# A sparse graph-attention kernel: batch order, gather columns and store placement near its end

## What is computed

```
h  = relu(layernorm(x)) @ W                       # 8192 x 128
e  = leaky_relu(h@a_src [:,None] + h@a_dst [None,:], 0.2)
e  = where(adj > 0, e, -9e15)
out = x + softmax(e, axis=1) @ h                  # a row without neighbours gets the mean of h
```

## Time and profile before

| | before |
|---|---|
| median of 3 runs, us | 804.62 |
| profiled execution, us (its span) | 803.09 (801.3) |
| busy: PE, DVE, ACT, POOL | 64%, 75%, 66%, 64% |
| DMA | 299.31 MB, mean 374 GB/s |
| last instruction on DVE before the final store starts | 793.30 us |

### The profile page before, as it was taken

The page is one execution under the profiler, slowest core; times in us unless marked ns, Lnnn a source line. Parts: engine busy times, 40 slices in busy tenths (PEclk is TensorE's granted clock), DMA queues, the critical chain, the costliest instruction groups (busy, mean ns, idle before and its releaser), DMA issues.

```text
span 801.3 us, 8973 instructions
## 1 busy us (share of the span) xinstructions
PE 516.1 (64%) x1855; PEld 233.0 (29%) x1855; DVE 602.0 (75%) x3125; ACT 527.0 (66%) x371; POOL 512.4 (64%) x522
## 2 busy tenths in 40 slices
PE   3786566677667667666657766676766666756521
PEld 3762223233222233232222222232322122222221
DVE  7957568766876768777779778777776798768984
ACT  3889667676766667676767767677666767676300
POOL 4753776665657665677667666656777656667771
PEclk9799756656765675876785676667667677676655
DMA  8999999999999999999999999999999999999410
GB/s 333 424 393 407 401 403 410 407 406 413 405 407 413 404 407 394 405 396 400 390 400 404 390 402 410 395 409 398 390 382 403 380 406 396 404 380 385 137 37 15
DMA packets 40904, 299.31 MB, mean 374 GB/s; under 512 B 11053, under 2 KB 14035, under 8 KB 24465
## 3 DMA queue, kind: packets, MB, share of 16 engines
q1 hardware_dynamic: 22976, 276.83, 85.5%
q0 software_dynamic: 15328, 17.58, 7.0%
q10 hardware_dynamic: 2544, 4.33, 1.6%
HBM read 304.31 MB, written 8.65 MB: 391 GB/s over the span
## 4 chain that ended last, share of the span: by engine, by line
DMA 70%; ACT 10%; issue 8%; DVE 8%; PE 3%; POOLq 0%; ACTq 0%; DVEq 0%
DMA adj_buf<-in_adj 69%; ACT mask_buf L467 9%; DVE x_all L821 3%; PE banks L1018 1%; DVE stats L560 1%; PE banks L1049 1%; ACT work L431 1%; PE banks L1008 1%; DMA x_all<-in_x 1%; ACT gathered L446 0%; DVE mv_all L564 0%; ACT work L441 0%; DVE newton L577 0%; DVE newton L579 0%; DVE rstd L581 0%
## 5 line engine op out<-in xcount | busy, mean ns | idle before, releaser
L467 ACT ACTIVATE mask_buf<-adj_buf,minus_half 128x2048 bf16<-128x2048 int32 x252 | 490.4, 1994 | 205.9 <-DMA adj_buf<-in_adj 205.4
L361 POOL DMA_INDIRECT gathered<-table,index x448 | 448.3, 1001 | 242.1 <-issue 145.5
L1049 PE MATMUL banks<-mask_buf,bit_ident 128*128 128x512 bf16 x1024 | 388.9, 528 | 103.5 <-ACT mask_buf L467 102.7
L1049 PEld LDWEIGHTS banks<-mask_buf,bit_ident 128*128 128x128 bf16 x1024 | 107.9, 124 | 329.2 <-ACT mask_buf L467 191.6
L821 DVE SCALAR_TENSOR_TENSOR x_all<-gathered,weight,x_all 128x128 f32<-128x128 f32 x512 | 157.7, 348 | 7.2
L636 DVE MAX8 words<-banks 128x8 f32<-128x512 f32 x64 | 44.7, 699 | 122.6 <-PE banks L1049 122.6
L1047 PE MATMUL banks<-key_rows,ones_b 3*128 3x512 bf16 x64 | 32.3, 504 | 124.0 <-ACT mask_buf L467 123.5
L1090 PE MATMUL banks<-x_all,one_hot 128*128 128x128 f32 x128 | 42.5, 433 | 17.5 <-DVE x_all L821 17.4
L1047 PEld LDWEIGHTS banks<-key_rows,ones_b 3*128 3x128 bf16 x64 | 6.1, 95 | 145.7 <-ACT mask_buf L467 144.2
L640 DVE MAX8 words<-rest 128x8 f32<-128x512 f32 x64 | 44.5, 695 | 2.2
L638 DVE MATCH_REPLACE8 rest<-words,banks 128x512 f32<-128x512 f32 x64 | 43.6, 681 | 0.0
(11 more groups left out here) (162 smaller groups left out, 536.1 us busy)
## 6 DMA issues: line engine op xcount, KB each, us to landing
adj_buf<-in_adj SPq DMA_DIRECT2D x128, 2048.0 KB, 18.7
gathered<-table,index POOLq DMA_INDIRECT x448, 6.4
table<-gathered ACTq DMA_DIRECT2D x4, 1040.0 KB, 14.7
x_all<-in_x SPq DMA_DIRECT2D x3, 1024.0 KB, 11.0
out<-x_all SPq DMA_DIRECT2D x2, 1280.0 KB, 23.2
x_all<-in_x SPq DMA_DIRECT2D x2, 512.0 KB, 5.3
out<-x_all SPq DMA_DIRECT2D x1, 1024.0 KB, 26.3
w_gathered<-table,w_index POOLq DMA_INDIRECT x24, 5.8
```

The costliest lines, as they stand in the source:

```text
L361: nc.gpsimd.indirect_dma_start(g_cols[buf][:, k, :], None, table, bass.IndirectOffsetOnAxis(index[:, buf, k:k + 1], 0), bounds_check=N, oo ...
L467: nc.scalar.activation(mask_buf[:, u], adj_buf[:, u], ACT.Sign, bias=minus_half[:]).then_inc(mask_ready, 1)
L1049: ins = mm(bank, bit_ident[:, h * PART_BITS + c], mask_buf[:, u, c * BIT_COLS:(c + 1) * BIT_COLS], start=False, stop=(h == PARTS - 1 and c ...
```

## The change

`BY_TILE` takes in batch 29. From batch 28 on (`CATCH_UP`) DVE sums batch i-2 and no longer i-3: batch 28 holds two sums, 25 and 26, and batch 31 none. The logits of batches 26 to 29 stand alone behind `make_records` of the batch after; ACT's softmax of batch i-2 stands behind unit 4 (in batch 28 behind unit 3). The last pair of units is loaded as one unit and two halves, each half masked and packed by itself. SP's stores wait for the last half. In batch 31 each tile has six gather columns and none is shared; neighbours from the seventh on make the node wide. After the loop, logits and placing stand between the steps of sums. Groups end with batches 10, 21 and 31 (before 9, 19, 31), and the first two groups' wide gathers are issued in threes over three batches. `wide_logits` waits for the sums first; `wide_sum` divides at its end and not at its start.

```diff
...
+CATCH_UP = 28
+WIDE_PARTS = ((0, 3), (3, 6), (6, 9))
+GROUP_ENDS = (10, 21, 31)
...
+BY_TILE = (29, 30, 31)
...
+        w_acc = [work[:, 1, 0, :], work[:, 1, 1, :]]
...
+            def load_part(i, u, lo, hi, loaded):
+                row = rows_of(adj, i * BATCH + u // PARTS, 1)[:, 0, :]
+                at = u % PARTS * PART
+                sp.dma_start(adj_buf[:, u, lo:hi], row[:, at + lo:at + hi]).then_inc(loaded, 16)
...
+                for u in range(0, UNITS - 2 if i == LAST else UNITS, 2):
...
+            sp.wait_ge(mask_ready, LAST * UNITS - 1)
+            load_part(LAST, UNITS - 2, 0, PART, adj_loaded[UNITS // 2 - 1])
+            sp.wait_ge(mask_ready, LAST * UNITS)
+            for h in range(2):
+                load_part(LAST, UNITS - 1, h * PART // 2, (h + 1) * PART // 2, end_loaded[h])
+            sp.wait_ge(end_loaded[1], 16)
...
-                    gather(buf, OWN, SLOTS, end_gathers_done[0])
...
-                    if i == GROUP_ENDS[g] + 3:
-                        wide_gather(g)
-            wide_gather(GROUPS - 1)
+                    for part, (lo, hi) in enumerate(WIDE_PARTS):
+                        if i == GROUP_ENDS[g] + 2 + part:
+                            wide_gather(g, lo, hi)
+            wide_gather(GROUPS - 1, 0, MORE + 1)
...
+            def mask_last():
+
+                act.wait_ge(part_packed, LAST * UNITS)
+                for h, signal in enumerate((end_masked, mask_ready)):
+                    act.wait_ge(end_loaded[h], 16)
+                    half = slice(h * PART // 2, (h + 1) * PART // 2)
+                    nc.scalar.activation(mask_buf[:, UNITS - 1, half], adj_buf[:, UNITS - 1, half], ACT.Sign,
+                                         bias=minus_half[:]).then_inc(signal, 1)
...
-                    mask(i, u)
-                    if u == 3 and i >= SUM_LAG:
+                    if i == LAST and u == UNITS - 1:
+                        mask_last()
+                    else:
+                        mask(i, u)
+                    if u == 3 and SUM_LAG <= i <= CATCH_UP:
                         softmax(i - SUM_LAG)
+                    if u == (3 if i == CATCH_UP else 4) and i >= CATCH_UP:
+                        softmax(i - 2)
                     for g in range(GROUPS - 1):
                         if u == 5 and i == GROUP_ENDS[g] + 7:
                             wide_softmax(g)
-                    if u == 6 and i == LAST:
-                        softmax(LAST - 2)
...
+                if i == LAST:
+                    ours, shared = (slice(0, OWN), slice(OWN, SLOTS)) if lo == 0 else (slice(SHARED, SLOTS), slice(0, SHARED))
+                    v.memset(valid[:, par, lo, shared], 0.0)
+                    done.add(v.tensor_scalar(valid[:, par, lo, ours], top[:, lo, 0:OWN], float(MEAN_KEY), None, ALU.is_ge))
+                    settled()
+                    next(beside, None)
+                    v.scalar_tensor_tensor(own, top[:, B, 0:OWN], -float(MEAN_KEY), skip[:, B, 0:OWN],
+                                           ALU.add, ALU.add).then_inc(index_ready, 1)
...
+                    v.tensor_copy(ninth[:], top[:, :, OWN])
+                    v.tensor_copy(rec[:, ring, :, 0:MORE], top[:, :, OWN:OWN + MORE])
+                    v.tensor_scalar(unfit[:, 4], top[:, :, OWN + MORE], float(EXP_BIAS), None, ALU.is_ge)
...
+            def later(rounds, steps):
+
+                for _ in range(rounds):
+                    yield
+                yield from steps
...
-                for k in range(SLOTS):
+                first = SHARED if i == LAST and lo else 0
+                for k in range(first, first + (OWN if i == LAST else SLOTS)):
...
-                dve.wait_ge(w_gathers, 16 * (MORE + 1) * (g + 1))
-                settled()
-                done.add(v.tensor_scalar(w_tmp[:, 0], w_gathered[:, :, D_COL], w_rec[:, REC_S:REC_S + 1], None, ALU.add))
-                settled()
-                done.add(v.scalar_tensor_tensor(w_tmp[:, 1], w_tmp[:, 0], ALPHA, w_tmp[:, 0], ALU.mult, ALU.max))
-                settled()
-                done.add(v.tensor_tensor(w_tmp[:, 0], w_tmp[:, 1], w_valid[:], ALU.mult))
-                settled()
-                done.add(v.tensor_scalar(w_tmp[:, 1], w_valid[:], 1.0, MASKED, ALU.subtract, ALU.mult))
-                settled()
-                done.add(v.tensor_tensor(w_score[:, 0:MORE], w_tmp[:, 0], w_tmp[:, 1], ALU.add))
-                settled()
 
                 dve.wait_ge(sums_closed, g + 1)
                 sums = banks[:, sums_banks[g], 0:SUMS]
                 done.add(v.tensor_copy(w_score[:, MORE:MORE + 1], sums[:, F:F + 1]))
+                dve.wait_ge(w_gathers, 16 * MORE * (g + 1))
+                settled()
+                done.add(v.tensor_scalar(w_tmp[:, 0], w_gathered[:, :, D_COL], w_rec[:, REC_S:REC_S + 1], None, ALU.add))
+                settled()
+                done.add(v.scalar_tensor_tensor(w_tmp[:, 1], w_tmp[:, 0], ALPHA, w_tmp[:, 0], ALU.mult, ALU.max))
+                settled()
+                done.add(v.tensor_tensor(w_score[:, 0:MORE], w_tmp[:, 1], w_masked[:], ALU.add))
                 settled()
                 v.tensor_reduce(w_m[:, 0:1], w_score[:], AX.X, ALU.max, negate=True).then_inc(w_logits, 1)
 
+                dve.wait_ge(w_x_gathered, 16 * (g + 1))
...
+                v.tensor_scalar(w_acc[0], w_gathered[:, 0, 0:F], w_prob[:, 0:1], None, ALU.mult)
+                v.tensor_scalar(w_acc[1], w_gathered[:, 1, 0:F], w_prob[:, 1:2], None, ALU.mult)
                 done.add(v.tensor_tensor(w_prob[:, MORE:MORE + 1], w_prob[:, MORE:MORE + 1], sums[:, F + 1:F + 2], ALU.mult))
                 settled()
+                add(0, 2)
+                add(1, 3)
...
+                done.add(add(0, MORE, w_first[:]))
+                settled()
+                done.add(v.tensor_tensor(w_acc[0], w_acc[0], w_acc[1], ALU.add))
+                settled()
+                v.scalar_tensor_tensor(w_x[:, g, :], w_acc[0], w_m[:, 1:2], w_x[:, g, :], ALU.mult, ALU.add
+                                       ).then_inc(w_out_ready, 1)
...
-            for i in range(LAST):
+            for i in range(BATCHES):
                 find_words(i, 0)
                 if i in BY_TILE:
                     decode(i, 0, 1)
-                if i >= SUM_LAG:
+                if CATCH_UP <= i < LAST:
+                    if i == CATCH_UP:
+                        weighted_sum(i - 3)
+                    weighted_sum(i - 2)
+                elif SUM_LAG <= i < CATCH_UP:
                     weighted_sum(i - SUM_LAG, beside=logits(i - LOGITS_LAG))
-                elif i >= LOGITS_LAG:
+                elif LOGITS_LAG <= i < SUM_LAG:
                     alone(logits(i - LOGITS_LAG))
                 find_words(i, 1)
                 decode(i, 1 if i in BY_TILE else 0, BATCH, beside=place_wide(i - COUNT_LAG) if i >= COUNT_LAG else ())
                 make_records(i)
+                if CATCH_UP - 1 <= i < LAST:
+                    alone(logits(i - 1))
                 wide_steps(i)
 
-            find_words(LAST, 0)
-            decode(LAST, 0, 1)
-            weighted_sum(LAST - 3, beside=logits(LAST - 2))
-            find_words(LAST, 1)
-            decode(LAST, 1, BATCH, beside=place_wide(LAST - 1))
-            make_records(LAST)
-            alone(logits(LAST - 1))
-            alone(place_wide(LAST))
+            weighted_sum(LAST - 2, beside=chain(logits(LAST - 1), place_wide(LAST)))
             done.add(v.tensor_tensor(unfit_all[:], unfit_all[:], unfit[:], ALU.max))
             settled()
             done.add(v.tensor_reduce(unfit_top[:], unfit_all[:], AX.XY, ALU.max))
             settled()
             v.tensor_scalar(unfit_top[:], unfit_top[:], 0.0, None, ALU.is_gt).then_inc(unfit_ready, 1)
-            weighted_sum(LAST - 2)
             wide_index(GROUPS - 1)
+            weighted_sum(LAST - 1, beside=logits(LAST, 0, 1))
+            weighted_sum(LAST, 0, 1, beside=later(4, logits(LAST, 1, BATCH)))
+            weighted_sum(LAST, 1, BATCH)
             dve.wait_ge(unfit_summed, 1)
             v.tensor_copy(unfit_n[:], banks[:, 2, 8:9]).then_inc(verdict, 1)
-            weighted_sum(LAST - 1)
-            alone(logits(LAST, 0, 1))
-            weighted_sum(LAST, 0, 1)
-            alone(logits(LAST, 1, BATCH))
-            weighted_sum(LAST, 1, BATCH)
             wide_logits(GROUPS - 1)
...
+                    if in_halves and c == PART_BITS // 2:
+                        pe.wait_ge(mask_ready, BATCHES * UNITS)
...
+                    if i == LAST and u == 4:
+                        add_sums(LAST - 3)
                 if i >= COUNT_LAG:
                     count_wide(i - COUNT_LAG)
-            add_sums(LAST - 3)
...
```

68 lines of the change are left out of this document (39 added, 29 removed).

## The result

The changed kernel takes 799.75 us, the median of four executions (798.42 to 800.10), against 804.85 for the kernel before beside it: a ratio of 0.9928 [0.9904, 0.9951]. (The quotient of the two medians is 0.9937, inside that interval.) The forecast was 799.4. The profiled pair differs by less: 803.09 to 800.10, spans 801.3 to 798.3.

What follows compares the result with a forecast made beforehand. Loads pace the stream; then the start of the last find_words and DVE's work behind it count. DVE's end moves from 793.59 to 788.4, 5.2 us less, so the median goes from 804.62 to 799.4; range 796.5 to 802.6.

Steps and rivals of the forecast that it cites:

- DVE's account: DVE from 671 us on: 10.8 us of added work against 12.7 idle, reaching the last find_words at 750.6.
- The softmax that holds the masks: ACT in batch 31 waits for batch 29's logits until 744.6; last mask ends 750.9, DVE starts 751.8.
- the 0.95 on PE: Halves of the last pair: two matmuls instead of four behind the last mask, 0.95 us instead of 1.93.
- Stores 0: SP's stores moved behind the last load: they delayed nothing before in ring order, so the move gives 0.
- gathers 0: POOL's gathers for batches 30 and 31 and the last group land in time: cost 0, at most 1.5 us.
- The tail: DVE's work from the last find_words at 751.8, summed piece by piece to an end at 788.4; before, 793.59.
- The close "not touched": Behind DVE's last instruction: 7.7 us for the store of group 2 and program end, taken as unchanged.
- Masks not held: Rival: DVE's debt is smaller, so ACT's last masks are not held; 2.1 us more won, 797.3; chance 0.15.
- Dearer pieces: Rival: DVE's decoding in the five crowded batches slows when it never idles; 2.4 us more, 801.8; chance 0.16.
- No change: Rival: dearer DVE pieces plus wide gathers 1.5 us late give 803.3, no change that can be told; chance 0.07.
- Slower by held gathers: Rival: stores behind the last load hold a gather that DVE awaits in sum 29's logits; 817.5; chance 0.05.

Runs made afterwards that it cites:

- p1: Changed kernel with the wide stores of groups 0 and 1 issued earlier, between batch 31's gathers: 799.36 us, ratio 0.9925 to the kernel before.
- e7: Changed kernel with the tail's logits and placing alone again, not between the steps of sums: 803.11 us, ratio 0.9976 to the kernel before.
- e1: Changed kernel with SP's stores issued behind the last load's issue, not waiting for the last half: 802.03 us, ratio 0.9948 to the kernel before.
- e5: Changed kernel with batch 31's two shared columns back (14 gathers, eight slots a row): 803.34 us, ratio 0.9966 to the kernel before.
- x2: Changed kernel with the nine wide gathers of groups 0 and 1 each issued in one go: 800.49 us, ratio 0.9934 to the kernel before.
- g1: Kernel before with only the new group boundaries (10, 21, 31) and wide gathers in threes: 807.54 us, ratio 1.0031 to the kernel before.
- x1: Changed kernel with the old group boundaries (9, 19, 31), gathers still in threes: 799.42 us, ratio 0.9919 to the kernel before.
- a1: Changed kernel measured once more with no edit: 800.94 us, ratio 0.9947 to the kernel before.
- b1: Changed kernel with old group boundaries and the last group's gathered-column scores ahead of copying PE's last sum: 796.25 us, ratio 0.9871 to the kernel before.
- e8: Changed kernel with the last group's gathered-column scores made ahead of the wait for PE's sums: 799.44 us, ratio 0.9926 to the kernel before.

## Why the prediction was right, and where it was not

- **DVE's account: right.** 10.8 us of new work on 12.7 of idle time was to bring DVE to the last words at 750.6. It was there at 749.79 (752.27 less the wait of 2.48), and from batch 28 to tile 0 of 31 it waited for PE nowhere.
- **The softmax that holds the masks: wrong.** It did not stand in batch 31, and in batch 30 it stood 1.15 us for some 2 expected. The last words start at 752.27 against 751.8 for two other reasons: the pair of units 4 and 5 came 1.8 later, and the halves did not give the 0.95 on PE. TensorE, kernel after:

```profile
744.89 1.89 PE L1108 MATMUL banks<-mask_buf,bit_ident 128*128 128x512 bf16 x4
746.57 0.63 PE L1149 MATMUL banks<-x_all,one_hot 128*128 128x128 f32 x2
746.99 0.42 PE L1150 MATMUL banks<-max_sum,one_hot 128*128 128x2 f32 x2
747.28 0.78 PE L1149 MATMUL banks<-x_all,one_hot 128*128 128x128 f32 x2
747.85 0.42 PE L1150 MATMUL banks<-max_sum,one_hot 128*128 128x2 f32 x2
748.13 4.03 PE L1108 MATMUL banks<-mask_buf,bit_ident 128*128 128x512 bf16 x12
```

  The f32 sums of a batch (746.57 to 748.13) now stand between the packing of units 4 and 5. Behind them PE has 12 matmuls to do in one go and ends at 752.16: it is behind ACT, and what the last mask is split into matters no more here. How fast it does them is a matter of its clock: 4.03 us in this run, 3.25 in p1, which starts its words 0.77 behind the last mask. So the halves gave PE nothing in this execution, and can have given it the forecast 0.95 in p1 and e7 (0.77 and 0.76 behind the last mask, 1.93 before). What the split gave ACT is unit 6 by itself: it landed at 744.64, the last half at 747.19. In one load with unit 7 its mask could have begun only at the second of these and the last mask ended near 751.2, an estimate, in place of 750.27. The kernel without the split was not run.
- **Stores 0, gathers 0: right.** e1 for the stores; no gather was waited for in the kernel after, and none in e5 with two more. Without the threes two gathers were late, ahead of the tail (x2). The store that took 26.3 to land takes 11.3 now:

```profile
out<-x_all SPq DMA_DIRECT2D x1, 1024.0 KB, 11.3
```

- **The tail: right, piece by piece.** Forecast and measured: words, decode, records 7.4 and 7.42; sum 29 with logits 30 and the placing 7.6 and 7.45; group index 0.9 and 0.90; sum 30 6.2 and 6.13; two tiles with their wait 6.45 and 6.12 (the wait of 0.3 did not come); PE 2.75 and 2.68; group logits 1.38 and 1.47; group sum 3.9 and 3.80. Together 36.6 and 35.97. e7 and e5 show what carries it: 3.0 from the interleaving, 2.5 from the six columns (2.4 by the prediction's own terms: 0.88 on the records, 0.76 on each tile). The two add up to a little more than the 5.13 that the tail lost; the group's logits and sum took 0.3 more than before (1.47 and 3.80 for 0.73 and 4.24).
- **The close "not touched": wrong, by 2.4 us.** This is the step that failed ("The 7.7 us behind it (store of group 2, end of program) are not touched"). 7.71 became 10.06, and the group boundaries, whose only price in the prediction was the work of group 1 in the crowded batches, do it (g1, x1). Nothing in the diff touches the last store's instruction.
- **Why the total fits all the same.** By the pieces: tail -5.13, close +2.35, last words 1.0 nearer to the arrival of the matrix (22.09 in place of 752.49 - 729.40 = 23.09; by the estimate above the split of the last pair can account for 0.9 of it): -3.8. The profiled pair shows -3.0, since the matrix came 0.8 later in the second. The medians show -5.1 and the ratio -5.8, with 1.9 to either side; in a1 the medians show -5.0 and the ratio -4.3, with 1.2 to either side. So some 4 to 5 us is what the change is worth, and part of the agreement is luck. The profiled execution of before, from which the sum was made, was faster than all that were timed, and the forecast put its median 1.53 above the profile; in the kernel after the median lies 0.35 below it. That hid 1.9 of the 2.2 by which the profiled time missed its forecast (800.10 for 797.9).
- **The rivals.** Masks not held: its mechanism came true and its price did not, for the two reasons above. Dearer pieces: refuted by the list of the tail. No change: refuted by the interval of the ratio, which ends at 0.9951. Slower by held gathers: refuted.

## What to carry to other kernels

Where an engine issues a tail alone, add it up piece by piece from starts in the trace: eight pieces came out within 0.33 us each. Then look behind the last instruction too: a stretch that the change "does not touch" needs a row that says what sets its length. The prediction had none, and the 2.4 us stood in the first pair of profiles, as end of span less end of DVE. By the rows of PE, splitting the last unit of a stream helps the engine that takes it up only if that engine is waiting at the moment.

## What the runs showed of the hardware

- GpSimd's closing drain behind an indirect store has a length that goes with GpSimd's program: 6.68 and 6.68 us in x1 and b1 and 6.84 in the kernel before (last group from batch 20), 9.21 in seven kernels, 9.26 in p1, 9.37 in g1 and e5 and 10.11 in x2 (last group from batch 22). It repeats to 0.01 us where kernels share GpSimd's program; two gathers more in batch 31 make it 0.16 longer (e5). The boundaries change both which rows the last store holds and what GpSimd had issued before; x2, with the rows of the kernel after and another order of the gathers, shows that the order has a part. What carries it was not found.
- The same 12 matmuls behind the same masks took 4.03 us in one execution and 3.25 in another, at granted clocks of 0.66 and 0.98 in the window from 748 to 752 us, though the program to that point differs by nothing on TensorE. With e7 and e8, which share every engine's program up to there, that moves the last words by 1.2 to 1.4 us from one execution to the next.
- The masks wait for one sixteenth of each load. From about 150 us on, in the kernels before and after, fifteen of a load's sixteen landing signals come within some 4 us and the sixteenth alone, 2 to 3 us behind them at first and 7 to 11 from 400 us on. The last half in the kernel after has the others by 740.00 and the last at 747.19. What holds it back is open. If that share were spread over all, the last landing would come some 6 us earlier, an estimate from these two times; no run tries it, and how much of it the masks would pass on is open.
